# Two expert stages: all experts for all tokens, against 46 tiles of tokens sorted by expert

## The chip, the cores and the metric

The kernel runs on one core of a Trainium2 chip. The metric is the device time of one execution in microseconds. A core has five engines that each work through their own instruction stream: TensorE (PE, with its weight loads shown apart as PEld), VectorE (DVE), ScalarE (ACT), GpSimd (POOL) and SyncE (SP, which here only issues DMAs). They are ordered against each other by semaphores alone.

## The reference

The reference is a network of eight stages on a residual of 4 batches of 1024 tokens of 128 features: attention, experts, a Mamba block, experts again, a sparse attention, a feed-forward stage, a delta-rule attention and a feed-forward stage. The change concerns the second and the fourth, which use the same weights:

```
logits = einsum('bsh,eh->bse', x, router_w)              # E = 8 experts, H = 128
probs = softmax(logits)
weights, indices = top_k(probs, 2)                       # K = 2 of 8
weights = weights / (weights.sum(-1) + 1e-06)
h13 = einsum('bsh,ehi->bsei', x, w13)                    # w13: 8 x 128 x 512
gate, up = split(h13, 2)                                 # 256 each
h = silu(gate) * up
y = einsum('bsei,eih->bseh', h, w2)                      # w2: 8 x 256 x 128
out = (take(y, indices) * weights).sum(over the 2)
```

Here x is the layer-normed residual, and the result is added to the residual. The reference computes all eight experts and uses two.

## The kernel before

The residual lies in SBUF as 32 tiles of 128 tokens (tokens on partitions). Each stage is a function that opens a block with one program for each engine; a stage ends when all engines have reached the end of its block. Operands of large products are split into two fp16 halves, high and low, and a product is three matmuls (`product_of_halves`, L246): high by high, high by low, low by high.

In `moe_stage` the work unit is a chunk of 512 tokens and one expert: 8 chunks x 8 experts = 64 units. `schedule()` yields one list of named pieces, and every engine walks through that same list and does the pieces that it knows; so the order on each engine is written out by hand, and the waits inside the pieces only delay. A unit j has these pieces. `up` (twice, for the two blocks of 128 hidden features): TensorE writes the gate and the value (6 matmuls of 512 columns each time), ScalarE takes Silu of the gate (L1226), VectorE multiplies it with the value into `exact` (L1313). `keep`: ScalarE rounds `exact` to the high half (L1234), GpSimd subtracts for the low half (L1250). `down`, two units later: TensorE makes 24 matmuls of 128 columns with token rows as output, and VectorE adds each tile of 128 tokens, scaled by the token's weight for this expert (zero for six of eight), to the residual (L1324). Between the units of a chunk, `ahead` places the preparation of the next batch: moments, root, norm (`apply`, L327), transposes (`turn`, L431, L416, L1214, L1261), router logits (L1158, L1277, L1278) and the choice of two experts (`choose`, L1281 to L1305), and for the first experts the split of their weights (L1201, L1267). Three buffers hold `exact`, gate and hidden halves.

At the start of the kernel, SP loads the first batch, the constants and the attention weights and then, in `load_rest`, the rest of the input, `expert_rank` and `router` (L84 to L86). The transfers that build attention's stacks follow it on the same queue: psi (L654), phi (L661, L669), the halves of q and k (L676), and the stacks (L691). GpSimd issues indirect DMAs in one place, the sparse stage (L2424), each with one row index for each of 128 partitions.

## Time and profile before

| | us |
|---|---|
| median of 3 runs | 3946.96 (3943.35 to 3953.65) |
| profiled execution, span from first to last instruction | 3942.5 |
| mean granted clock of TensorE in it | 0.872 |
| PE busy | 3249.7 (82%) |
| DVE busy | 2818.9 (72%) |
| ACT busy | 2313.5 (59%) |
| POOL busy | 1237.5 (31%) |

The page gives no time for the profiled execution other than its span; the median of the runs is 4.5 us above it. The page also cuts the span into 40 slices; the expert stages are the two stretches in which TensorE's digit is 9 and its granted clock 9 (slices 9 to 11, and 18 to 20). A busy share is the time an engine's instructions take; a granted clock of 1.00 is TensorE at 2.4 GHz, of 0.50 at 1.2 GHz, and values between are a mean of the two levels over the stretch.

### The profile page before, as it was taken

What the parts mean: (1) busy time and instruction counts of PE and PEld (TensorE: products, weight loads), DVE (VectorE), ACT (ScalarE), POOL (GpSimd) and SP (SyncE); (2) the same over time, 40 slices, a digit from 0 to 9 for tenths busy, and PEclk for the clock granted to TensorE, in tenths of its full rate; (3) what the DMA queues carried; (4) which work ended last, traced back from release to release, by engine and by line L of the source; (5) the groups of instructions that cost most, each with busy time, mean ns of one, the idle gap of its engine ahead of it and who ended that gap; (6) DMA issues with size and microseconds to landing.
All of it is one profiled execution on the core that took longest, in us unless ns stands there. A gap on an engine that the chain in (4) does not pass through costs nothing. (4 is left out here: it accounts for less than half of the span.)

```text
span 3942.5 us, 87849 instructions
## 1 busy us (share of the span) xinstructions
PE 3249.7 (82%) x36196; PEld 1488.6 (38%) x36256; DVE 2818.9 (72%) x4293; ACT 2313.5 (59%) x3870; POOL 1237.5 (31%) x1018
## 2 busy tenths in 40 slices
PE   6999999899867677689988888887995676776799
PEld 1222222266411122156533333333453555554445
DVE  8898899587679998887746767655445667656643
ACT  3888888766444555266542566665655564543565
POOL 1100100055436776645533000001004565452100
PEclk7999999999967778799999999998997676656799
...
DMA packets 136019, 84.34 MB, mean 21 GB/s; under 512 B 92386, under 2 KB 107539, under 8 KB 135491
## 3 DMA queue, kind: packets, MB, share of 16 engines
...
q10 hardware_dynamic: 64, 0.07, 0.0%
...
## 5 line engine op out<-in xcount | busy, mean ns | idle before, releaser
L989 DVE TENSOR_REDUCE attn_peak_halves<-attn_ps 128x2 f32<-128x1024 f32 x512 | 601.5, 1218 | 58.5 <-PE attn_ps L820 50.7
L942 ACT ACTIVATE attn_weights<-attn_ps 128x512 f32<-128x512 f32 x1024 | 531.0, 601 | 101.4 <-PE attn_ps L848 101.3
L2974 DVE TENSOR_REDUCE sparse_peak<-sparse_ps 128x4 f32<-128x1024 f32 x256 | 309.6, 1223 | 136.3 <-PE sparse_ps L2600 134.5
L1250 POOL TENSOR_TENSOR moe_hidden<-moe_exact,moe_hidden 128x512 f16<-128x512 f32 x256 | 296.7, 1162 | 330.7 <-ACT moe_hidden L1234 322.0
L3672 POOL TENSOR_TENSOR delta_q<-delta_q,delta_weighted 128x512 f32<-128x512 f32 x240 | 324.1, 1377 | 235.4 <-ACT delta_weighted L4066 235.3
L2827 ACT ACTIVATE sparse_weights<-sparse_ps 128x512 f32<-128x512 f32 (+1 forms) x512 | 272.0, 585 | 173.8 <-PE sparse_ps L2667 87.9
L246 PE MATMUL moe_ps<-moe_xT_halves,moe_w_halves 128*128 128x512 f16 x1536 | 363.8, 384 | 9.4 <-DVE moe_w_halves L1267 5.9
L1772 POOL TENSOR_TENSOR mamba_out_c<-mamba_states,mamba_c_rep 128x1024 f32<-128x1024 f32 x128 | 301.4, 2367 | 176.8 <-DVE mamba_states L1839 138.5
L848 PE MATMUL attn_ps<-attn_q_stack,attn_k_stack 50*128 50x512 f16 x1024 | 321.9, 386 | 29.9 <-ACT attn_weights L942 7.1
L246 PE MATMUL ffn_ps<-ffn_layers,ffn_h_halves 128*128 128x512 f16 x1536 | 334.5, 379 | 3.6 <-ACT ffn_gate L3219 3.6
L1558 PE MATMUL mamba_ps<-mamba_stack,mamba_spread 96*128 96x512 bf16 x512 | 196.2, 493 | 157.3 <-ACT mamba_decays L1726 85.7
L1839 DVE TENSOR_TENSOR_SCAN mamba_states<-mamba_decays,mamba_ps 128x1024 f32<-128x1024 f32 x128 | 292.7, 2287 | 26.3 <-ACT mamba_decays L1726 10.1
L820 PE MATMUL attn_ps<-attn_k_stack,attn_q_stack 48*128 48x512 f16 x1024 | 271.2, 396 | 13.9 <-DVE attn_peak_halves L989 12.6
L3291 DVE TENSOR_TENSOR ffn_layers<-ffn_exact,ffn_layers 128x512 f16<-128x512 f32 x192 | 132.5, 692 | 204.8 <-ACT ffn_layers L3208 204.3
L860 PE MATMUL attn_ps<-attn_weights,attn_values 128*9 128x512 f32 x2048 | 270.3, 600 | 0.0
L1726 ACT ACTIVATE mamba_decays<-mamba_ps,mamba_rates 128x1024 f32<-128x1024 f32 x128 | 141.9, 1113 | 179.4 <-PE mamba_ps L1558 177.4
L1226 ACT ACTIVATE moe_gate<-moe_ps 128x512 f32<-128x512 f32 x256 | 152.0, 594 | 138.4 <-PE moe_ps L246 134.4
L1313 DVE SCALAR_TENSOR_TENSOR moe_exact<-moe_ps,moe_gate 128x512 f32<-128x512 f32 x256 | 174.5, 684 | 78.4 <-ACT moe_gate L1226 72.4
L848 PEld LDWEIGHTS attn_ps<-attn_q_stack,attn_k_stack 50*128 50x128 f16 x1024 | 80.6, 94 | 375.1 <-ACT attn_weights L942 284.4
L246 PEld LDWEIGHTS ffn_ps<-ffn_layers,ffn_h_halves 128*128 128x128 f16 x1536 | 149.9, 98 | 184.4 <-issue 4.5
L246 PE MATMUL moe_ps<-moe_w_halves,moe_hidden 128*128 128x128 f16 x3072 | 193.7, 220 | 18.2 <-POOL moe_hidden L1250 13.6
L246 PEld LDWEIGHTS moe_ps<-moe_xT_halves,moe_w_halves 128*128 128x128 f16 x1536 | 145.0, 99 | 164.5 <-DVE moe_w_halves L1267 8.0
...
## 6 DMA issues: line engine op xcount, KB each, us to landing
mamba_stack<-mamba_parts SPq DMA_DIRECT2D x96, 128.0 KB, 2.4
...
attn_q_stack<-attn_peak_rows SPq DMA_DIRECT2D x128, 2.0 KB
```

The lines of the kernel that those rows point to most:

```text
L246: made = pe.matmul(out, a, b, start=first and i == 0, stop=last and i == 2)
L820: made = pe.matmul(use.slot[:, p, :], q_stack[rows, slot, couple, t * P:(t + 1) * P], k_stack[rows, slot, couple, half_of(keys)], start=Tr ...
L848: pe.matmul(use.slot, k_stack[rows, slot, couple, k * P:(k + 1) * P], q_stack[rows, slot, couple, half_of(half)], start=True, stop=True).t ...
L860: made = pe.matmul(out_acc[32 * h:32 * h + HD + 1, :], values[:, b % 2, k, first + h, :], weights[:, step_no(g, half, k) % 2, h, :], start ...
L942: act.activation(weights[:, at % 2, h, :], use.slot, ACT.Exp).then_inc(*key_act.one())
L989: dve.tensor_reduce(peak_halves[:, turn % PEAKS, keys, at:at + 2], use.slot, AX_X, ALU.max).then_inc(*score_dve.one())
L1250: pool.tensor_tensor(low, exact_sb[:, i % 3, :], hidden[:, i // EB % 3, i % EB, 0, :], ALU.subtract).then_inc(*hidden_low.one())
L1772: pool.tensor_tensor(out_c[:, n % PRODUCTS, :], states[:, n % HELD, :], c_rep[:, b % 2, :], ALU.mult).then_inc(*product_made.one())
L1839: dve.tensor_tensor_scan(states[:, n % HELD, :], decays[:, n % DECAYS, :], mine, 0.0, ALU.mult, ALU.add).then_inc(*scanned.one())
L2827: act.activation(weights[:, at % 2, h, begin:], use.slot[:, begin:], ACT.Exp).then_inc(*key_act.one())
L2974: dve.tensor_reduce(peak[:, at % PEAKS, unit // 2, 4 * r:4 * r + 4], use.slot.rearrange("p h (a k) -> p (h a) k", a=2), AX_X, ALU.max).the ...
L3672: pool.tensor_tensor(so_far, so_far, weighted[:, half, :], ALU.add).then_inc(*long_added.one())
```

## The change

The two expert stages compute each token only for its two experts. In each stage:

- All four batches are prepared before the first product (`prepare`): norm, transposes, logits and choice as before, and `halve` makes a row of 256 fp16 values (high and low half) for each token. Batches 0 and 1 form lot 0, batches 2 and 3 lot 1 (`LOTS`).
- `rank` counts, by matmuls of the membership matrix with a triangular and a full matrix of ones, how many tokens of each expert stand before each token of the lot. `place_lot` turns this into a slot number for each token's first and second choice, where each expert's list begins at a multiple of 256, and into a table of which expert each tile of 256 slots belongs to. A lot has 2 x 2048 / 256 + 7 = 23 tiles, whatever the counts, so 46 in all.
- GpSimd writes the rows to `sorted_x` in HBM, by one indirect DMA for each 128 tokens and choice (32 for each lot, 64 in all).
- A tile j: SP loads its 256 rows (6 buffers), TensorE turns them with an fp16 identity (4 matmuls of 128 columns), ScalarE copies them, TensorE reads the expert's address from the table into a register (`value_load`) and makes 12 matmuls of 256 columns and, two steps later, 12 of 128 columns, all with the weights `parts` addressed by that register. ScalarE does Silu, the high half and the copy of the result; VectorE the product and the low half (which was GpSimd's); SP stores 256 result rows of fp32 to `sorted_y`.
- When all tiles of a lot are stored, GpSimd gathers each token's two result rows (again 64 indirect DMAs in all), and VectorE adds them, scaled, to the residual (`combine`).
- `load_rest` zeroes both lists `sorted_x` once, at the start of the kernel. Two constants are loaded at the start of each expert stage. The semaphores `zeroed`, `scattered` and `gathered` are the kernel's own for its whole length.

```diff
         sp.dma_start(self.router[:], self.dram["router"]).then_inc(*self.rest_in.dma())
+        for lot in self.sorted_x:
+            n = lot.shape[0] // SLOTS_E
+            sp.dma_start(lot.rearrange("(n p s) d -> p n (s d)", p=P, s=SB), self.dram["e_zeros"].unsqueeze(1).broadcast_to(
+                [P, n, SB * 2 * P])).then_inc(*self.zeroed.dma())
...
+SB = SLOTS_E // P
+LOTS = ((0, 2), (2, 4))
+PER_EXPERT = 2 * HIDDEN_E * 2 + EB * P * 2
+LOW13, HIGH2, LOW2 = 2 * HIDDEN_E, 4 * HIDDEN_E, 4 * HIDDEN_E + EB * P
+LIMITS = 16
+lot_tiles = lambda g: (LOTS[g][1] - LOTS[g][0]) * T * 2 // SLOTS_E + EXPERTS - 1
+LOT_STARTS = [sum(lot_tiles(n) for n in range(g)) for g in range(len(LOTS) + 1)]
+MOE_TILES = LOT_STARTS[-1]
...
+        def prepare(b):
+
+            yield "apply", b, 0
+            yield "turn", b, 0
+            yield "apply", b, 1
+            yield "turn", b, 1
+            yield "halve", b
+            yield "logits", b
+            yield "raise", b
+            yield "choose", b, 0
+            yield "choose", b, 1
+            if b + 1 == LOTS[lot_of(b)][1]:
+                yield "rank", lot_of(b)
+                yield "place", lot_of(b)
+            yield "weigh", b
...
+            early = [b for b in range(B) if lot_of(b) < 2]
+            for n, b in enumerate(early):
+                yield from prepare(b)
+                if n == 0:
+                    for other in range(1, B):
+                        yield "moments", other, 0
+                        yield "moments", other, 1
+                        yield "root", other
+                for e_ in range(n * EXPERTS // len(early), (n + 1) * EXPERTS // len(early)):
+                    yield "split", e_
+            late = [piece for b in range(B) if lot_of(b) >= 2 for piece in prepare(b)]
+            yield "gather_tile", 0
+            total_steps = MOE_TILES + 4
+            for j in range(total_steps):
+                if 1 <= j <= MOE_TILES:
+                    yield "high", j - 1
+                if 3 <= j < MOE_TILES + 3:
+                    yield "keep", j - 3
+                if j + 1 < MOE_TILES:
+                    yield "gather_tile", j + 1
+                if 1 <= j <= MOE_TILES:
+                    yield "low", j - 1
+                if j < MOE_TILES:
+                    yield "up", j
+                if 2 <= j < MOE_TILES + 2:
+                    yield "down", j - 2
+                if late and j >= 1:
+                    yield late.pop(0)
+                if j == LOT_STARTS[2] + 2:
+                    for c in range(HALVES * LOTS[0][0], HALVES * LOTS[0][1]):
+                        yield "combine", c
+            for c in range(HALVES * LOTS[0][1], CHUNKS):
+                yield "combine", c
+                if c == HALVES * TAKEN - 1:
                     yield ("next_root",)
                     yield ("next_inverse",)
...
+                def load(j):
+                    g = lot_of_tile(j)
+                    at = (j - LOT_STARTS[g]) * SLOTS_E
+                    if j == LOT_STARTS[g]:
+                        sp.wait_ge(*scattered[g].at(16 * 2 * span(g)))
+                    if j >= LOADED:
+                        sp.wait_ge(*turned_tile.at(j - LOADED + 1))
+                    sp.dma_start(sorted_in[:, j % LOADED], net.sorted_x[g][at:at + SLOTS_E].rearrange(
+                        "(p s) d -> p s d", s=SB)).then_inc(*loaded[j % LOADED].dma())
+
+                def store(j):
+                    g = lot_of_tile(j)
+                    at = (j - LOT_STARTS[g]) * SLOTS_E
+                    sp.wait_ge(*y_taken.at(j + 1))
+                    sp.dma_start(net.sorted_y[g][at:at + SLOTS_E].rearrange("(p s) d -> p s d", s=SB),
+                                 y_sb[:, j % STORED]).then_inc(*stored[j % STORED].dma())
+
+                for j in range(MOE_TILES + LOADED):
+                    if j < MOE_TILES:
+                        load(j)
+                    if j >= LOADED:
+                        store(j - LOADED)
+                for n in range(STORED):
...
+                def gather_tile(j):
+                    if j == 0:
+                        pe.wait_ge(*prepared.at(1))
+                    pe.wait_ge(*loaded[j % LOADED].at(16 * (j // LOADED + 1)))
+                    if j:
+                        pe.wait_ge(*taken.at(j))
+                    for half in range(2):
+                        for s in range(SB):
+                            at = half * SLOTS_E + s * P
+                            made = pe.matmul(ps[:, 0, at:at + P], sorted_in[:, j % LOADED, s, half * P:(half + 1) * P],
+                                             ident_half[:], start=True, stop=True)
+                    made.then_inc(*turned_tile.one())
...
+                def up(j):
+                    g = lot_of_tile(j)
+                    if j == 0:
+                        pe.wait_ge(*weights_low.at(2 * EXPERTS))
+                    if j == LOT_STARTS[g]:
+                        pe.wait_ge(*tabled.at(g + 1))
+                    value[j] = pe.value_load(expert_at[0:1, j:j + 1], min_val=0, max_val=(EXPERTS - 1) * PER_EXPERT)
+                    pe.wait_ge(*taken.at(j + 1))
+                    source = sorted_T[:, j % 2, 0, :], sorted_T[:, j % 2, 1, :]
+                    for which, (bank, empty, full) in enumerate(((gate_bank(j), gated, gate_full),
+                                                                 (value_bank(j), exact_made, value_full))):
+                        if j >= 2:
+                            pe.wait_ge(*empty.at(j - 1))
+                        for k in range(EB):
+                            at = which * HIDDEN_E + k * P
+                            made = product_of_halves(pe, bank[:, k * SLOTS_E:(k + 1) * SLOTS_E],
+                                                     (parts[:, bass.ds(value[j] + at, P)],
+                                                      parts[:, bass.ds(value[j] + (LOW13 + at), P)]), source)
+                        made.then_inc(*full.one())
...
+                def gather_tile(j):
+                    act.wait_ge(*turned_tile.at(j + 1))
+                    if j >= 2:
+                        act.wait_ge(*value_full.at(j - 1))
+                    act.copy(sorted_T[:, j % 2].rearrange("p h n -> p (h n)"), ps[:, 0, :]).then_inc(*taken.one())
+
+                def up(j):
+                    if j >= 2:
+                        act.wait_ge(*exact_made.at(j - 1))
+                    act.wait_ge(*gate_full.at(j + 1))
+                    act.activation(gate_sb[:, j % 2, :], gate_bank(j), ACT.Silu, scale=1.0 / W_SCALE).then_inc(*gated.one())
+
+                def high(j):
+                    if j >= KEPT:
+                        act.wait_ge(*out_full.at(j - KEPT + 1))
+                    act.wait_ge(*exact_made.at(j + 1))
+                    act.copy(hidden[:, j % KEPT, 0].rearrange("p k n -> p (k n)"),
+                             exact_sb[:, j % 2, :]).then_inc(*hidden_high.one())
+
+                def keep(j):
+                    act.wait_ge(*out_full.at(j + 1))
+                    if j >= STORED:
+                        act.wait_ge(*stored[j % STORED].at(16 * (j // STORED)))
+                    act.copy(y_sb[:, j % STORED].rearrange("p s d -> p (s d)"), out_bank).then_inc(*y_taken.one())
+
+                pieces = {"root": lambda b: norm.root(act, b), "prepare_consts": prepare_consts, "split": split, "turn": turn,
+                          "halve": halve, "raise": raise_, "gather_tile": gather_tile, "up": up, "high": high, "keep": keep,
+                          "next_root": lambda: norm.root_next(act)}
                 for piece, *at in schedule():
                     if piece in pieces:
                         pieces[piece](*at)
 
...
             def _(pool):
-                for i in range(EB * units):
-                    pool.wait_ge(*hidden_high.at(i + 1))
-                    low = hidden[:, i // EB % 3, i % EB, 1, :]
-                    if i // EB >= 3:
-                        pool.wait_ge(*out_full.at(i // EB - 2))
-                    pool.tensor_tensor(low, exact_sb[:, i % 3, :], hidden[:, i // EB % 3, i % EB, 0, :],
-                                       ALU.subtract).then_inc(*hidden_low.one())
+                def scatter(b):
+                    g = lot_of(b)
+                    pool.wait_ge(*tokens_low.at(b + 1))
+                    pool.wait_ge(*placed.at(g + 1))
+                    for t in range(b * TPB, (b + 1) * TPB):
+                        for k in range(2):
+                            pool.indirect_dma_start(net.sorted_x[g], bass.IndirectOffsetOnAxis(slot_at[:, k, t:t + 1], 0),
+                                                    rows[:, t].rearrange("p h d -> p (h d)"),
+                                                    None).then_inc(*scattered[g].dma())
+
+                def gather(c):
+                    g = lot_of(c // HALVES)
+                    if c == HALVES * LOTS[g][0]:
+                        for n in range(STORED):
+                            pool.wait_ge(*stored[n].at(16 * len(range(n, LOT_STARTS[g + 1], STORED))))
+                    for t in range(c * TPC, (c + 1) * TPC):
+                        for k in range(2):
+                            pool.indirect_dma_start(found[:, t, k, :], None, net.sorted_y[g], bass.IndirectOffsetOnAxis(
+                                slot_at[:, k, t:t + 1], 0)).then_inc(*gathered[c].dma())
+
+                pool.wait_ge(*net.zeroed.at(16 * len(LOTS)))
+                for b in range(B):
+                    scatter(b)
+                for c in range(CHUNKS):
...
+                def place_lot(g):
+                    n, tiles = span(g), slice(LOTS[g][0] * TPB, LOTS[g][1] * TPB)
+                    limits = steps_in[:, 0:LIMITS].unsqueeze(1).broadcast_to([P, EXPERTS, LIMITS])
+                    counts = rank_bank(g)[:, n * EXPERTS:]
+                    before = rank_bank(g)[:, 0:n * EXPERTS].rearrange("p (t e) -> p t e", e=EXPERTS)
+                    dve.wait_ge(*ranked.at(g + 1))
+                    if g == 0:
+                        dve.wait_ge(*consts_in.at(32))
+                    settle(dve.tensor_tensor(over[:], counts.unsqueeze(2).broadcast_to([P, EXPERTS, LIMITS]), limits, ALU.is_gt))
+                    settle(dve.tensor_reduce(ends[:, 0, :], over[:], AX_X, ALU.add))
+                    settle(dve.tensor_tensor_scan(ends[:, 1, :], ones[:], ends[:, 0, :], 0.0, ALU.mult, ALU.add))
+                    settle(dve.tensor_tensor(ends[:, 2, :], ends[:, 1, :], ends[:, 0, :], ALU.subtract))
+                    made = dve.scalar_tensor_tensor(place[:, tiles], ends[:, 2, :].unsqueeze(1).broadcast_to([P, n, EXPERTS]),
+                                                    float(SLOTS_E), before, ALU.mult, ALU.add)
+                    made.then_inc(*based.one())
+                    dve.wait_ge(*based.at(g + 1))
+                    for k, picks in enumerate((chosen, runner)):
+                        settle(dve.tensor_tensor(key[:, tiles], picks[:, tiles], place[:, tiles], ALU.mult))
+                        settle(dve.tensor_reduce(slot[:, k, tiles], key[:, tiles], AX_X, ALU.add))
+                    dve.tensor_copy(slot_at[:, :, tiles], slot[:, :, tiles]).then_inc(*placed.one())
+                    lot, m = slice(LOT_STARTS[g], LOT_STARTS[g + 1]), lot_tiles(g)
+                    settle(dve.tensor_tensor(passed[:, lot], ends[0:1, 1, :].unsqueeze(1).broadcast_to([1, m, EXPERTS]),
...
+                def low(j):
+                    dve.wait_ge(*hidden_high.at(j + 1))
+                    dve.tensor_tensor(hidden[:, j % KEPT, 1].rearrange("p k n -> p (k n)"), exact_sb[:, j % 2, :],
+                                      hidden[:, j % KEPT, 0].rearrange("p k n -> p (k n)"),
+                                      ALU.subtract).then_inc(*hidden_low.one())
+
+                def combine(c):
+                    dve.wait_ge(*gathered[c].at(16 * 2 * TPC))
+                    for k in range(2):
+                        for t in range(c * TPC, (c + 1) * TPC):
+                            x = net.residual[:, t, :]
+                            made = dve.scalar_tensor_tensor(x, found[:, t, k, :], share[:, k, t:t + 1], x, ALU.mult, ALU.add)
+                        made.then_inc(*added.one())
+                        dve.wait_ge(*added.now())
+                    if c < HALVES * TAKEN:
+                        norm.take_next_moments(dve, c)
```

## Rows read from the trace of the kernel before

**Rows 1.** The page, busy us (share of the span) and instructions of each engine.
```profile
PE 3249.7 (82%) x36196; PEld 1488.6 (38%) x36256; DVE 2818.9 (72%) x4293; ACT 2313.5 (59%) x3870; POOL 1237.5 (31%) x1018
```

**Rows 2.** Timeline, first expert stage's edges: start, duration, instruction, idle before it.
```profile
765.61 0.35 SPq L1140 DMA_DIRECT2D moe_w<-in_w  x1
...
768.77 2.14 DVE L327 TENSOR_SCALAR moe_xn<-residual,w_ln_moments,w_ln_inv 128x128 f32<-128x128 f32 x8
...
772.39 0.57 ACT L416 COPY moe_xT<-moe_ps 128x512 f32<-128x512 f32 x1
...
773.26 4.58 PE L246 MATMUL moe_ps<-moe_xT_halves,moe_w_halves 128*128 128x512 f16 x12 [1.19 <-DVE moe_xT_halves L1261]
...
1054.32 0.34 SPq L1536 DMA_DIRECT2D mamba_w_in<-in_m_w_in  x1
```

**Rows 3.** Busy us of each engine in a stretch, clock, DMA share, GB/s.
```profile
855.00:955.00 100.00, 95.71 (x865) 61.26 (x864) 78.78 (x221) 65.83 (x112) 55.97 (x49) 1.00 0.01 1
```

**Rows 4.** Timeline of one unit in the steady state.
```profile
1041.60 1.50 PE L246 MATMUL moe_ps<-moe_w_halves,moe_hidden 128*128 128x128 f16 x24
1042.94 2.75 PE L246 MATMUL moe_ps<-moe_xT_halves,moe_w_halves 128*128 128x512 f16 x12
1045.53 1.50 PE L246 MATMUL moe_ps<-moe_w_halves,moe_hidden 128*128 128x128 f16 x24
...
1043.14 1.13 DVE L1324 SCALAR_TENSOR_TENSOR residual<-moe_ps,moe_weights,residual 128x128 f32<-128x128 f32 x4 [0.54 <-PE moe_ps L246]
1043.85 0.60 ACT L1226 ACTIVATE moe_gate<-moe_ps 128x512 f32<-128x512 f32 x1 [1.52 <-PE moe_ps L246]
1044.55 0.69 DVE L1313 SCALAR_TENSOR_TENSOR moe_exact<-moe_ps,moe_gate 128x512 f32<-128x512 f32 x1 [0.27 <-ACT moe_gate L1226]
```

**Rows 5.** Instructions by line (ns min/median/max, first and last start), and one of the timeline.
```profile
L1214 ACT ACTIVATE moe_xT_halves<-moe_xT x16: 629/630/631, 771.9 to 1865.8; 128x512 f16<-128x512 f32 x16
...
L980 DVE TENSOR_TENSOR attn_phi_parts<-attn_sums,attn_phi_parts x1: 1226/1226/1226, 14.6 to 14.6; 128x1024 f16<-128x1024 f32 x1
...
770.83 1.02 DVE L1267 SCALAR_TENSOR_TENSOR moe_w_halves<-moe_w,moe_w_halves 128x512 f16<-128x512 f32 x2
```

**Rows 6.** Small VectorE operations of the choice by line; norms, grouped (busy us, mean ns).
```profile
L1282 DVE TENSOR_TENSOR moe_key<-moe_probs,moe_total x8: 828/1056/1066, 785.2 to 1876.9; 128x64 f32<-128x64 f32 x8
L1282 DVE TENSOR_TENSOR moe_key<-moe_left,moe_second x8: 224/225/226, 787.9 to 1881.8; 128x64 f32<-128x64 f32 x8
...
L327 DVE TENSOR_SCALAR moe_xn<-residual,w_ln_moments,w_ln_inv 128x128 f32<-128x128 f32 x32 | 14.5, 514 | 0.1
```

**Rows 7.** GpSimd's indirect DMAs in the sparse stage; their landing; a 128 KB DMA.
```profile
2083.20 1.12 POOL L2424 DMA_INDIRECT sparse_gathered_k<-sp_table_k,sparse_row_at  x1 [15.09 <-DVE sparse_row_at L2966]
2084.62 0.99 POOL L2424 DMA_INDIRECT sparse_gathered_v<-sp_table_v,sparse_row_at  x1 [0.30 <-issue]
2085.59 6.58 POOL L2415 DMA_DIRECT2D sparse_k_stack<-sp_halves  x12
...
DMA to landing us min/median/max: 2.7/2.8/3.8
...
mamba_stack<-mamba_parts SPq DMA_DIRECT2D x96, 128.0 KB, 2.4
```

**Rows 8.** A ScalarE copy of 128 columns out of PSUM.
```profile
L927 ACT COPY attn_bias_row<-attn_ps x1: 278/278/278, 25.8 to 25.8; 128x128 f32<-128x128 f32 x1
```

**Rows 9.** Busy us by stretch as in rows 3: Mamba stage, sparse stage.
```profile
1200.00:1300.00 100.00, 71.97 (x228) 16.13 (x228) 91.20 (x57) 55.26 (x53) 75.77 (x34) 0.74 0.07 16
...
2200.00:2300.00 100.00, 87.18 (x1072) 34.15 (x1085) 66.97 (x56) 68.13 (x134) 7.72 (x23) 0.98 0.04 11
```

**Rows 10.** Start of the kernel: router load, first attention scores, busiest DMA stretch.
```profile
12.94 0.43 SPq L86 DMA_DIRECT2D w_router<-in_router  x1
...
38.70 0.61 PE L820 MATMUL attn_ps<-attn_k_stack,attn_q_stack 48*128 48x512 f16 x2
...
6.00:17.00 11.00, 5.32 (x12) 2.94 (x13) 7.95 (x27) 3.92 (x6) 0.38 (x1) 1.00 0.91 267
```

318 lines of the change are left out of this document (151 added, 167 removed).

## The prediction

> **What bounds the kernel now.** I read the page first: TensorE is busy 82% of a 3942.5 us span and no other engine comes near it over the whole [rows 1]. A whole-kernel share says nothing about two stages out of eight, so next comes the timeline at their edges. The first expert stage runs from 765.61 to the first DMA of the stage after it at 1054.32, 288.7 us [rows 2]; the second repeats the pattern from 1675.67 to 1964.92, 289.3 us. The first product of an expert begins at 773.26, so only 7.65 us are preparation. The busy times of the stretch 855 to 955 show the steady state: TensorE 95.7 of 100 us at a granted clock of 1.00, VectorE 79, ScalarE 66, GpSimd 56 [rows 3]. The timeline of a unit (one chunk of 512 tokens, one expert) repeats every 1045.53 - 1041.60 = 3.93 us, with 24 products of 128 columns in 1.50 us and 12 of 512 in 2.75 us, back to back [rows 4]. 64 units of 3.93 are 251 us. TensorE alone bounds these stages; the other engines fit inside its time.
>
> **What the change removes.** All 8 experts are computed for all 4096 tokens now, and two are used. Afterwards 46 tiles of 256 tokens are computed. Per tile there are 12 products of 256 columns, 12 of 128 and 4 of 128 (turning the loaded rows). A product of 512 columns takes 2.75/12 = 0.229 us and one of 128 takes 1.50/24 = 0.0625 [rows 4]; halfway by columns, 256 costs 0.118. The tile is 12 x 0.118 + 16 x 0.0625 = 2.41 us, and 46 tiles are 111 us of TensorE in place of 251. The 140 us saved are the whole gain. The rest of this part is what is paid for them, in the order of the stage.
>
> **Preparation, now in front of everything.** Lot 0 needs batches 0 and 1 normed, routed and ranked before a single token can be placed, where the kernel before prepares batches 1 to 3 beside the products. Up to the first applied norm it is as now, 3.16 us (765.61 to 768.77) [rows 2]. A batch then runs serially: 8 norms 2.14 us; from their end to the copy of the turned half 2.05 us (770.91 to 772.96) [rows 2, 5]; the high half of 1024 columns on ScalarE, twice the 0.63 of 512, 1.26; the low half on VectorE 1.23; two operations on logits 0.5, Exp with its hop 0.35, and 15 small operations of the choice at 0.225 plus about 0.04 between them, 3.9 [rows 5, 6]. That is 11.5. To it come the weighing of batch 0 (4 small operations, 1.0), the moments of three batches (2.4 each, which is 3.16 less 0.7 for root and reciprocal, 7.2), two experts' weights split (1.02 each on VectorE, 2.0) [rows 5], batch 1 (11.5), the ranking by 17 small products (1.5), and place_lot up to its slots, 10 settled operations of 64 to 128 elements at about 0.3 (3.0). Sum 3.2 + 11.5 + 1.0 + 7.2 + 2.0 + 11.5 + 1.5 + 3.0 = 40.9 us. The logits' products on TensorE lie beside the halving. The 1.5 and the 3.0 are estimates from those small operations, good to a microsecond.
>
> **Scatter.** 32 indirect DMAs of GpSimd place lot 0. The trace has eight, in four pairs: from start to start 1.42 us in two of them, 1.32 in the others, of which 0.99 to 1.12 is the instruction and 0.30 lies between the two; they land after 2.8 [rows 7]. The rows moved there are twice as long, the count of 128 rows is the same. I take 1.37: 32 x 1.37 = 43.8 us. Bounds: 0.97, the time from the second of a pair to the plain DMA behind it, and 2.2, which is 1.37 with the 0.83 us added that a small VectorE operation took more beside GpSimd (1056 ns against 225) [rows 6]. At 0.97 the stage gains 26 us on this forecast, if nothing else holds it, and at 2.2 it loses 27. All of it is on the path, since the first tile waits for the whole lot's semaphore. Then 2.8 to land, 0.35 to issue the load and 2.4 for 128 KB [rows 2, 7], 1.0 for turning and copying: 40.9 + 43.8 + 6.6 = 91.3 us. Nothing of the tiles can start earlier. What VectorE does meanwhile (batches 2 and 3, the other six experts, about 39 us) ends near 80 us and is hidden, and would come out only if the scatter took less than about 33 us. Lot 1's 32 scatters (to about 129 us) and lot 0's 32 gathers lie beside tiles and cost nothing, unless GpSimd is late by over 40 us.
>
> **Pace of a tile.** TensorE could do 2.41 us. ScalarE now has four operations: 0.60 for Silu, 0.63 for the high half, 0.57 for the copy of the turned rows, about 0.38 for the result's 256 columns (between 0.28 for 128 and 0.57 for 512) [rows 2, 4, 5, 8]. But in its order `high` of tile j-1 comes first in step j, and it waits for VectorE's product, which waits for the Silu that ScalarE did last. The cycle is Silu 0.60, hop 0.10 (1044.45 to 1044.55), product 0.69, hop 0.10, high 0.63, result copy 0.38, turned copy 0.57, and 0.03 between each of four: 3.2 us. The rings of three to six buffers don't break it, since it is an order on one engine. Below it lies 2.41. Above it lies TensorE at its lower clock: 5120 columns at 1.2 GHz are 4.27 us, 4.5 with the issue. The granted clock was 0.74 where TensorE was busy 72% and 0.98 at 87% [rows 9]; at 2.41 of 3.2, 75%, the new stage lies between these. Each tile also loads a register from SBUF on TensorE's queue and addresses 24 operands by it, which no row of this trace prices; by the nearest bounds it costs nothing while TensorE's 0.8 us of slack hide it, and the pace is 4.5 when they don't. I take 3.5, a tenth over the cycle and nearest to it. 46 tiles and three steps of drain: 49 x 3.5 = 171.5 us, to 262.8.
>
> **After the last tile.** Its store takes 2.8 (issue and 128 KB), then lot 1's 32 gathers 43.8, all exposed because the first waits for every store of the lot; 2.8 to land and 8 combining operations 2.3, from four in 1.13 [rows 4]. 262.8 + 51.7 = 314.5 us, against 288.7 and 289.3: slower by 25.5 a stage, 51 for both. Residual additions of the kernel before (256 operations of 0.34 per stage) become 64, and GpSimd's 128 subtractions go to VectorE; neither bounded and neither will.
>
> **The zeroed lists.** 46 tiles x 256 rows x 512 B = 6.03 MB are written at the start on SP's queue, behind the router's load (its DMA is issued at 12.94 us) and ahead of psi, phi and the stacks that the first scores need (38.70) [rows 10]. The busiest stretch moved 267 GB/s at 0.91 of the queues, so it takes 23 us. The DMAs behind it were issued from 13.4 to 30.1 with waits in between; redone behind a queue that is free at 36, the stacks land near 47 to 52, 8 to 14 us after 38.70. Bounds: 0, if the small transfers find a way around, and 26, if HBM to HBM runs at half the rate. I take 14. The second stage pays nothing here.
>
> **Sum.** 51 + 14 = 65 us. The profiled execution has a span of 3942.5; the page gives no time around it, and the median of the three timed runs is 3947.0, 4.5 above. On the span the sum is 4008, as a time 4012 us.
>
> One rule of the Trainium skill speaks against this change. Rows first: a small VectorE operation on 64 columns took 1056 ns where its twin took 225, and the norms of 128 columns took 514 ns in the mean in a stage where GpSimd is busy half the time, against 0.27 a piece in the first eight, before GpSimd begins [rows 2, 6]. SBUF — State Buffer, "Who interferes with whom", says that VectorE in its two-port modes (copy, cast, tensor_scalar) takes the port pair it shares with GpSimd for the whole instruction, and that a DMA of GpSimd is then starved of descriptor time. The norms of batches 2 and 3 are tensor_scalar, and run beside lot 0's scatter. The trace agrees as far as it shows the two engines holding each other up; it has no indirect DMA beside a norm. By that rule the scatter would go as in the last rival below; without it, 1.37 stands.
>
> **The rivals.**
> - Tile pace set by TensorE's queue (register loads, register addresses, the lower clock): 4.5 us a tile. For it: the clock of 0.74 at 72% busy, and the serial waits of the queue. Against: 0.98 at 87% [rows 9]. 49 x 1.0 more per stage, 98 for both: 4110 us.
> - The other side: TensorE keeps the pace, 2.41 us, as it does now at clock 1.00. For it: GpSimd and VectorE are light in the tiles, and TensorE has been the one bound of the stage [rows 3]. Against: the ScalarE cycle, written out above, which needs ScalarE to do two tiles at once. 49 x 1.09 less, 107 for both: 3905 us. Faster begins at a pace of 3.5 - 65/98 = 2.84 us.
> - Indirect DMAs of 2.2 us in the first scatter, where VectorE prepares beside it: 32 x 0.83 = 27 a stage, 53 for both: 4065 us. For it: [rows 6]. Against: the low count of two-port operations, 16 norms and a few copies in those 44 us.
>
> **How the numbers follow.** The forecast gets 0.45, with a range of its own of 3970 to 4060 (pace 3.18 to 3.9, zeros 0 to 26); TensorE's queue 0.18; the other side 0.24; slow scatters 0.10; 0.03 lies within 0.3%, about what a measurement of this kernel can tell from no change. Range 3900 to 4115: down to the fast case, up to the slow one, which leaves out the combinations of several costs and any bigger gain. Faster 0.25, same 0.03, slower 0.72.
>
> **What would show it.** In the changed profile: first product of an expert about 91 us after the stage's first DMA (right if 80 to 100); DMA_INDIRECT 128 times a stage with 1.3 to 1.4 between starts and 32 of them after the last store; Silu to Silu 3.2 to 3.9 us with ScalarE's `high` waiting for VectorE; granted clock of the tiles between 0.6 and 1; first scores at 47 to 53 us. The prediction is wrong if Silu to Silu is under 2.84, if a gather or scatter costs well under 1 us, or if the loads of registers show as TensorE waiting a microsecond or more in each tile.

## The result, and the profile of the changed kernel

| | time (us) | ratio to before, 95% interval |
|---|---|---|
| before | 3947.57 (3943.35 to 3953.65) | |
| changed | 4087.11 (4079.35 to 4094.62) | 1.0355 [1.0334, 1.0376] |

Forecast was 4012, so the sign was right, and the forecast cost, 65 us, was under half of the 139.5 measured. The page of the changed kernel, beside [rows 1]: TensorE has shed 245 us of work and the span is 135 us longer.

```profile
span 4077.5 us, 84371 instructions
...
PE 3005.2 (74%) x34232; PEld 1387.9 (34%) x34292; DVE 2653.2 (65%) x3877; ACT 2174.6 (53%) x3696; POOL 1190.8 (29%) x1018
```

The first expert stage now runs from SP's first DMA at 774.53 to that of the Mamba stage at 1126.34, 351.8 us against 288.7 [rows 2]; the second from 1750.02 to 2104.70, 354.7 against 289.3. GpSimd's timeline gives the edges of its four bursts of 32 indirect DMAs (only the first of each burst is shown; within one, nearly all starts are 1.25 to 1.27 apart, a few up to 1.76, and the last ones start at 858.99, 909.57, 1020.08 and 1117.25):

```profile
818.46 1.21 POOL L1370 DMA_INDIRECT sorted_x<-moe_rows,moe_slot_at  x1 [87.31 <-DVE moe_slot_at L1472]
...
870.30 0.96 POOL L1370 DMA_INDIRECT sorted_x<-moe_rows,moe_slot_at  x1 [10.34 <-DVE moe_slot_at L1472]
...
980.50 1.42 POOL L1381 DMA_INDIRECT moe_found<-sorted_y,moe_slot_at  x1 [69.97 <-DMA sorted_y<-moe_y]
...
1078.21 0.95 POOL L1381 DMA_INDIRECT moe_found<-sorted_y,moe_slot_at  x1 [57.18 <-DMA sorted_y<-moe_y]
```

Busy times cut at these edges and at the tiles' own (columns as in [rows 3]: length, busy us of PE, PEld, DVE, ACT, POOL, granted clock, DMA share, GB/s):

```profile
774.50:818.50 44.00, 12.49 (x65) 10.98 (x65) 30.08 (x145) 14.57 (x25) 0.04 (x1) 0.50 0.24 74
818.50:861.00 42.50, 11.40 (x48) 9.84 (x48) 15.98 (x53) 6.14 (x11) 32.01 (x32) 0.50 0.16 50
861.00:881.50 20.50, 9.42 (x76) 7.37 (x77) 10.77 (x39) 6.06 (x11) 8.70 (x9) 0.57 0.24 72
881.50:915.50 34.00, 4.76 (x22) 1.76 (x19) 1.40 (x2) 1.81 (x4) 22.09 (x23) 0.56 0.15 46
915.50:986.00 70.50, 62.58 (x699) 52.78 (x700) 35.54 (x52) 48.24 (x102) 4.40 (x4) 0.95 0.32 98
986.00:1025.00 39.00, 4.47 (x34) 2.37 (x31) 1.83 (x3) 2.27 (x5) 26.67 (x28) 0.61 0.20 56
1025.00:1078.00 53.00, 43.70 (x480) 36.83 (x480) 28.29 (x56) 33.97 (x71) 0.00 (x0) 0.92 0.27 84
1078.00:1122.50 44.50, 0.00 (x0) 0.00 (x0) 20.96 (x93) 0.31 (x1) 30.53 (x32) 0.50 0.18 47
```

The fourth and sixth lines are the finding. Lot 1's scatters lie in 881.5 to 915.5 and lot 0's gathers in 986 to 1025, and there hardly any engine but GpSimd works: TensorE 4.8 of 34 us and 4.5 of 39. Between them TensorE is busy 62.6 of 70.5. TensorE's timeline of the first band shows how it goes on, for long nothing and then one product at a time, waiting for nothing that the profile shows ("issue"):

```profile
881.06 0.84 PE L251 MATMUL moe_ps<-moe_parts,moe_hidden 128*128 x8
883.08 0.22 PE L251 MATMUL moe_ps<-moe_parts,moe_hidden 128*128 x1 [1.18 <-issue]
883.81 0.22 PE L251 MATMUL moe_ps<-moe_parts,moe_hidden 128*128 x1 [0.51 <-issue]
885.22 0.22 PE L251 MATMUL moe_ps<-moe_parts,moe_hidden 128*128 x1 [1.19 <-issue]
887.34 0.26 PE L251 MATMUL moe_ps<-moe_parts,moe_hidden 128*128 x1 [1.91 <-issue]
901.44 0.59 PE L1261 MATMUL moe_ps<-moe_ident_half,moe_sorted_in 128*128 128x128 f16 x4 [13.84 <-issue]
...
907.73 0.37 PE L251 MATMUL moe_ps<-moe_sorted_T,moe_parts 128*128 128x256 f16 x1 [2.44 <-issue]
910.52 0.37 PE L251 MATMUL moe_ps<-moe_sorted_T,moe_parts 128*128 128x256 f16 x1 [2.42 <-issue]
```

The single products start about 0.70 us or a multiple of it apart (0.73, 1.41, 2.12 and 2.79 in these lines), where those of 256 columns are 0.11 apart in the steady tiles. But a large part of each band is one standstill: 13.84 us here, and 28.26 in front of the product at 1025.31 in the second. The others wait for TensorE. The same thing stands in the first burst, with no tile, no register and no load of SP's near it. TensorE's products for batch 3's logits start between 840.48 and 843.67 and their signal (a semaphore event of the trace) comes at 860.74, 0.8 us after the burst's last DMA; VectorE, which waits for it, stands 18.23 us (the releaser printed had long been done):

```profile
841.31 1.23 DVE L1409 TENSOR_TENSOR moe_rows<-moe_xn,moe_rows 128x1024 f16<-128x1024 f32 x1 [2.83 <-ACT moe_rows L1324]
860.76 0.23 DVE L1419 TENSOR_REDUCE moe_best<-moe_ps 128x8 f32<-128x64 f32 x1 [18.23 <-DMA attn_sums<-in_tables]
```

So these products had started by the trace, and what is missing is their end. The band has it too. The four products that turn tile 3 start at 879.04; their signal stands in the trace at 900.68, 21.3 us after the recorded end of the last of them, where it comes 0.01 after it in the steady tiles, and ScalarE's copy, which waits for it, starts at once:

```profile
879.04 0.39 PE L1261 MATMUL moe_ps<-moe_ident_half,moe_sorted_in 128*128 128x128 f16 x4
900.71 0.59 ACT L1334 CAST moe_sorted_T<-moe_ps 128x512 f16<-128x512 f32 x1 [6.34 <-remote]
```

Away from bursts a tile repeats every 929.88 - 927.19 = 2.69 us. ScalarE's timeline shows the cycle of the prediction, with `high` waiting 0.81 for VectorE's product:

```profile
927.19 0.61 ACT L1340 ACTIVATE moe_gate<-moe_ps 128x512 f32<-128x512 f32 x1
928.61 0.62 ACT L1346 CAST moe_hidden<-moe_exact 128x512 f16<-128x512 f32 x1 [0.81 <-DVE moe_exact L1486]
929.14 0.37 ACT L1353 COPY moe_y<-moe_ps 128x256 f32<-128x256 f32 x1
929.40 0.59 ACT L1334 CAST moe_sorted_T<-moe_ps 128x512 f16<-128x512 f32 x1
929.88 0.61 ACT L1340 ACTIVATE moe_gate<-moe_ps 128x512 f32<-128x512 f32 x1
```

And the zeroed lists move the first scores from 38.70 [rows 10] to:

```profile
45.31 1.03 PE L825 MATMUL attn_ps<-attn_k_stack,attn_q_stack 48*128 48x512 f16 x4 [6.62 <-DMA attn_k_stack<-attn_halves]
```

That is not their whole cost. The expert stage behind attention starts 8.9 us later than before (774.53 against 765.61). In the other runs that zero at the start it is 5.9 to 19.0 us (771.51 to 784.65), and none in those that don't, or that do it later (763.70 to 765.38).

### The profile page after: what moved, and what is told of

Its sections match the earlier page's. It is cut to its first block and busy times, and to the rows that moved or that the text cites. A ratio compares the mean times of both kernels' runs of the same rounds, so it can differ in the third digit from the quotient of the medians.

```text
span 4077.5 us, 84371 instructions
## 1 busy us (share of the span) xinstructions
PE 3005.2 (74%) x34232; PEld 1387.9 (34%) x34292; DVE 2653.2 (65%) x3877; ACT 2174.6 (53%) x3696; POOL 1190.8 (29%) x1018
## 5 line engine op out<-in xcount | busy, mean ns | idle before, releaser
L3465 DVE TENSOR_TENSOR ffn_layers<-ffn_exact,ffn_layers 128x512 f16<-128x512 f32 x192 | 132.7, 692 | 204.7 <-ACT ffn_layers L3382 204.2
L1381 POOL DMA_INDIRECT moe_found<-sorted_y,moe_slot_at x128 | 123.5, 965 | 291.9 <-DMA sorted_y<-moe_y 254.1
L4240 ACT ACTIVATE delta_weighted<-delta_v,delta_fir_w 128x512 f32<-128x512 f32 x240 | 168.7, 721 | 61.9 <-POOL delta_q L3846 61.0
L251 PE MATMUL moe_ps<-moe_sorted_T,moe_parts 128*128 128x256 f16 x1104 | 153.0, 289 | 59.5 <-issue 48.3
L1486 DVE SCALAR_TENSOR_TENSOR moe_exact<-moe_ps,moe_gate 128x512 f32<-128x512 f32 x92 | 63.6, 692 | 204.3 <-ACT moe_gate L1340 139.7
L1370 POOL DMA_INDIRECT sorted_x<-moe_rows,moe_slot_at x128 | 125.0, 976 | 203.9 <-DVE moe_slot_at L1472 166.1
L771 POOL TENSOR_SCALAR attn_peak_parts<-attn_peak 128x16 f16<-128x16 f32 x32 | 8.3, 261 | 550.5 <-DVE attn_peak L1000 550.5
```

The source lines that it names most:

```text
L251: made = pe.matmul(out, a, b, start=first and i == 0, stop=last and i == 2)
```

## The experiments

Every run edits the changed kernel or repeats a kernel unchanged, but for bursts_row and bursts_plain, which edit the kernel before. The theory: a burst of back-to-back indirect DMAs of GpSimd holds the other engines up. Rivals: the register-addressed weights, the traffic, the tiles' own order. Each run names the chip that it ran on, which came to matter. The kernel before took a median between 3944.6 and 3949.2 us on all six chips, so it doesn't tell them apart. The chip of the first measurement above isn't recorded; it shows the bands.

### Chip 1: take the overlap away, or the register

**serial** keeps everything of GpSimd's away from tiles.

```
-  if j == LOT_STARTS[g]:
-      sp.wait_ge(*scattered[g].at(16 * 2 * span(g)))
+  if j == 0:
+      for lot in range(len(LOTS)):
+          sp.wait_ge(*scattered[lot].at(16 * 2 * span(lot)))
...
-  if c == HALVES * LOTS[g][0]: ...  # lot g stored
+  if c == 0: ...                    # all tiles stored
```

> Nothing of GpSimd's lies beside tiles any more: tile 0's load waits for both lots' 64 scatters, and all 64 gathers wait for the last store. Theory (a burst of back-to-back indirect DMAs holds the other engines up, so that what lies beside it gains nothing): both bands of about 36 us without tiles go, two bands of 40.5 us of exposed scatters and 40 us of exposed gathers come; a stage is 96 + 40.5 + 5.5 + 49 x 2.69 + 3 + 80 + 5 = 362 us against 348, so about 4115 us. Rival (the bands come from the tiles' own order, from the change of lots or from the buffers): they stay and the exposed DMAs are added, 4240 us or more. By the prediction's own belief (bursts beside tiles cost nothing) it would be 4087 + 2 x 80 = 4247 us.

4115.79 us, ratio 1.0432 [1.0401, 1.0464], as the theory had it (4115). All 46 tiles run in one stretch, TensorE busy 114 of 138 us, and none of it is lost:

```profile
860.00:917.00 57.00, 1.22 (x17) 1.14 (x17) 9.64 (x38) 1.91 (x5) 37.65 (x40) 0.50 0.14 45
917.00:1055.00 138.00, 114.06 (x1288) 95.89 (x1288) 63.66 (x92) 89.52 (x186) 1.24 (x3) 0.95 0.29 90
1055.00:1140.00 85.00, 0.00 (x0) 0.00 (x0) 19.97 (x88) 0.00 (x0) 59.80 (x63) 0.50 0.19 49
```

Putting 64 DMAs per stage (81 us) beside tiles had gained 29 us for two stages, not 160. The tiles' order and buffers are cleared.

**static** makes the weight addresses constants.

```
-  value[j] = pe.value_load(expert_at[0:1, j:j + 1], ...)
+  value[j] = (j % EXPERTS) * PER_EXPERT
```

> TensorE's weight addresses are constants (expert j mod 8 for tile j): it loads no register, and the tiles do not use the weights of their tokens' expert. Rival (register loads and addressed operands are what is slow beside the bursts): the bands without tiles go, about 3940 us, tiles keep their 2.7 us pace beside the bursts. Theory (the bursts hold up whatever the engines run): the bands stay as long as they were, 36 us each, and the time is 4087 within 10 us, because the register instructions were hidden in the steady pace.

4068.97 us, 1.0314 [1.0285, 1.0342], 18 less than the changed kernel, where I had allowed 10. The bands stay. The windows below are those of the changed kernel, and this stage starts 7.1 us later, so they catch some of the running tiles. Fairer is what the starts of Silu are apart beyond 2.69 us, summed over a stage: 68 us here, 74 in the changed kernel. Registers account for at most the 18 us gained, 9 a stage, about 6 of them in the bands.

```profile
881.50:915.50 34.00, 8.12 (x63) 5.20 (x60) 3.46 (x5) 4.02 (x8) 25.93 (x27) 0.59 0.19 59
986.00:1025.00 39.00, 8.92 (x65) 5.54 (x63) 3.71 (x6) 4.76 (x9) 27.55 (x29) 0.60 0.25 68
```

### Chip 1: pace the bursts

**paced2** and **paced6of8** make each pair wait for the Silu of one more tile; **passed_waits** adds a wait that is always met; **spaced4** puts a memset of 0.95 us behind every fourth DMA.

```
   for t in ...:
+      pool.wait_ge(*gated.at(t - 15))                    # paced2, lot 1's scatters
+      pool.wait_ge(*gated.at(t - 15 + (t - 16) // 3))    # paced6of8
+      pool.wait_ge(*placed.at(1))                        # passed_waits
       for k in range(2):
           pool.indirect_dma_start(...)
+      if t % 2: settle(pool.memset(idle[:], 0.0))        # spaced4
```

> GpSimd waits for ScalarE's silu of one more tile ahead of every two indirect DMAs of lot 1's scatters and of lot 0's gathers: 2.5 us of DMA in each 2.69 us tile, so a gap of 0.2 us only. Theory: the engines are held up only while GpSimd issues without a pause, and a wait that follows their progress cannot run them dry for 30 us; if a gap of 0.2 us is enough, the two bands of about 36 us go and the time is about 3940 us; if a gap must be longer, tiles and DMAs take turns, and it is between 3990 and 4087 us. Rival (the DMAs' traffic makes the tiles' loads late): the rate of the traffic is nearly the same, so the time stays within 20 us of 4087.

> As the one before with every fourth tile left free: six DMAs and then a pause of about 3 us, 32 DMAs over 21 tiles. Theory (a pause lets the others catch up): no band without tiles, a stage of 348 - 75 = 273 us, 3937 us in all, less than before the change (3947). If six DMAs in a row are already too many: some us lost in each run of six, 3960 to 4040 us. Rival (traffic): three quarters of the rate, still some 60 us lost of 150, about 4030 us.

> The changed kernel with a semaphore wait of GpSimd ahead of each pair of indirect DMAs that is always met already: the bursts stay as dense, only their instruction stream is broken by a wait every 2.5 us. If the paced kernels were cured by the break in the stream (an instruction between the DMAs at which GpSimd lets others go), the bands without tiles vanish here too: about 3945 us. If they were cured by the pauses or by GpSimd following the tiles, the time stays at 4087 within 15 us.

> The changed kernel with a GpSimd memset of 0.95 us (own tile) after every four indirect DMAs, in all bursts: pauses that follow nobody's progress. A burst of 32 takes 32 x 1.26 + 8 x 1.2 = 50 us instead of 40. If a pause of about 1 us every 5 us is what the others need, the two bands of 36 us per stage go (-150 us) and the exposed bursts grow (first scatters and last gathers 10 us each, twice: +40 us): about 3975 us. If the feedback from the tiles is needed (GpSimd waiting when they fall behind), the bands stay and grow with the burst: about 4087 + 40 + 20 = 4150 us.

paced2 3988.90 (1.0111 [1.0078, 1.0143]), paced6of8 3991.52 (1.0111 [1.0089, 1.0134]): 98 and 96 us gained. passed_waits 4086.25 (1.0350 [1.0303, 1.0396]): nothing. spaced4 4026.12 (1.0197 [1.0148, 1.0247]): 61 gained, between the 3975 and the 4150 that I expected, though the pauses lengthen the four exposed bursts by 28 (46 to 47 us in place of 39 to 41). So the break must be a pause, not an instruction. That one which follows the tiles does better isn't shown: the paced bursts also paused more (32 DMAs in 57.4 and 52.2 us in paced2, 47 in spaced4, 39 to 40 unbroken).

The rival of traffic predicted 4087 within 20 for paced2 on the ground of an equal rate. The rate came out a quarter to a third lower, so this run alone doesn't rule it out. A loss in proportion to the rate would be some 110 of the 147 us of the bands, though, and 50 are left; and chip 5 below carries the same rows at full rate without loss. Both paced kernels missed the 3940 of the theory. In paced2 every second or third tile beside the pairs loses mostly 1.4 to 2.4 us (Silu 905.18 to 910.16 against 2.69), 24 and 26 us a stage:

```profile
902.50 0.61 ACT L1340 ACTIVATE moe_gate<-moe_ps 128x512 f32<-128x512 f32 x1
905.18 0.61 ACT L1340 ACTIVATE moe_gate<-moe_ps 128x512 f32<-128x512 f32 x1
910.16 0.62 ACT L1340 ACTIVATE moe_gate<-moe_ps 128x512 f32<-128x512 f32 x1
```

### The same bursts beside the dense stages

GpSimd issues 64 row DMAs beside the tiles of each dense stage (static addresses, no loads). bursts_row: rows of the input, index 0 everywhere, in the second dense stage with an operation of GpSimd after every four; bursts_plain: not indirect, in the second dense stage issued by SyncE. Both edit the kernel before. real_rows edits the changed kernel: the expert stage's slots, gathers from the result lists in the first dense stage and scatters in the second.

```
+  for n in range(64):
+      pool.indirect_dma_start(fetched[:, n, :], None, table, IndirectOffsetOnAxis(row_at[:, 0:1], 0))    # bursts_row
+      pool.dma_start(fetched[:, n, :], table[n * 16:n * 16 + P])                                        # bursts_plain
+      pool.indirect_dma_start(fetched[:, n, :], None, net.sorted_y[g], ...net.slot_at[:, k, t:t + 1])    # real_rows
```

> The kernel before, with 64 indirect row gathers of 128 rows of 512 B on the otherwise idle GpSimd beside the tiles of each dense stage (static weight addresses, no loads of the tiles' own; the fetched rows are not used): in the first dense stage back to back, in the second with one GpSimd elementwise operation of about 1.3 us after every four. Theory (back-to-back indirect DMAs starve TensorE of instructions, which come in blocks of 16 KB; a dense stage uses up some 12 TensorE instructions per us): TensorE runs on for 20 to 40 us and then all but stops until the burst of 80 us ends: 40 to 60 us lost in the first dense stage, under 10 us in the second: about 3997 us. Rival (only tiles with register-addressed weights, or tiles that load from DRAM, suffer): nothing lost in either, 3947 within 10 us. Rival (the traffic of the row DMAs is what disturbs): both stages lose, the second at four fifths of the rate nearly as much as the first.

> As the one before, other DMAs of the same bytes (128 rows of 512 B each, 64 of them back to back, consecutive rows, not used): in the first dense stage plain transfers issued by GpSimd, in the second the same transfers issued by SyncE on its own queue. If GpSimd's making of descriptors is the cause, the first dense stage loses as with indirect DMAs when they follow each other as closely (40 to 60 us), and the second nothing, about 3997 us; if it is the indirect form alone, neither loses, 3947 within 10 us; if it is the traffic of 64 KB every 1.3 us, the second stage loses as well, or more, since SyncE issues one every 0.4 us: over 3980 us.

> The changed kernel with bursts of 64 indirect DMAs beside the tiles of both dense stages, this time with the real slots of the second expert stage as rows: gathers of 512 B rows in the first dense stage, scatters of 512 B rows in the second (results unused). In the run before, with every index 0, TensorE kept its full pace beside such a burst for 80 us. If what holds TensorE up in the expert stages is the kind of rows (distinct rows spread over DRAM, packets that land within 3 us), the dense stages now lose 30 to 60 us each: 4087 + 60 to 120 = about 4170 us. If it is something of the expert stages' own code (instruction rate, its many waits), the dense stages lose under 10 us: about 4095 us.

bursts_row (chip 9) 3956.24, 1.0015 [0.9996, 1.0033]; bursts_plain (chip 9) 3947.16, 0.9994 [0.9978, 1.0011]; real_rows (chip 1) 4240.12, one run, 153 us over the changed kernel. Its first dense stage, from the burst's start at 2902.73 to its end at 2983:

```profile
2903.00:2923.00 20.00, 18.51 (x84) 7.96 (x83) 6.33 (x22) 7.06 (x11) 15.43 (x16) 1.00 0.20 50
2923.00:2983.00 60.00, 11.64 (x27) 2.52 (x25) 3.68 (x18) 6.49 (x9) 45.37 (x49) 0.54 0.19 52
2983.00:2988.00 5.00, 1.16 (x3) 0.23 (x3) 0.75 (x1) 0.00 (x0) 0.42 (x1) 0.56 0.07 21
2988.00:3020.00 32.00, 28.85 (x159) 14.11 (x159) 15.76 (x30) 20.17 (x31) 0.00 (x0) 0.86 0.00 1
```

The bands are no property of the expert stages: 20 us into a burst nearly everything stops here too. The DMA engines are 0.19 busy meanwhile, so it is no lack of bandwidth. In bursts_row they were 0.90 busy (128 reads of one row land after 15.9 us) and TensorE worked through:

```profile
2750.00:2785.00 35.00, 33.23 (x155) 14.87 (x153) 19.34 (x60) 23.43 (x35) 26.77 (x28) 1.00 0.86 41
2785.00:2830.00 45.00, 45.00 (x289) 24.32 (x288) 22.71 (x40) 28.90 (x44) 34.09 (x36) 1.00 0.90 40
```

I took this for proof that distinct rows decide. It was not: between the two runs the rows, the table, the kernel around them and the chip had changed.

### Which chip

**zero_rows** and **real_gaps** were to separate row, table, form and gap. Both are the changed kernel with other bursts in the dense stages (index 0 of the result lists, then plain transfers; the real slots with a short GpSimd operation after every second, then after every eighth gather), and their expert stages are unchanged, with unbroken bursts of 32.

> The changed kernel with 64 row DMAs beside the tiles of each dense stage again. First dense stage: indirect gathers from the same result lists as in the run that stopped everything, but with index 0 in all rows. Second: plain transfers issued by GpSimd that read 128 distinct rows, 16 KB apart, from these lists. If distinct rows matter only with the indirect form, neither stage loses, 4087 within 15 us. If distinct, scattered rows through GpSimd's queue are enough in any form, the second loses 20 to 60 us. If it was the table (lists in DRAM that the kernel itself owns, not an input) and not the index, the first loses about 75 us.

> The changed kernel with 64 indirect gathers by the real slots beside the tiles of each dense stage, and a small GpSimd operation with its semaphore (a gap of some 0.7 us) after every second gather in the first dense stage, after every eighth in the second. Unbroken, such bursts cost the two dense stages 153 us in all. If a gap of 0.7 us lets the engines through, whoever's progress it follows, a gap every 2.5 us cures the first (loss under 10 us) and one every 10 us leaves part of the loss in the second (10 to 60 us): 4110 to 4150 us. If only waiting for the tiles cures, both lose 70 us or more: 4230 us or more.

Chip 5: zero_rows 3928.00, real_gaps 3932.26 (one run each; before 3944.58 there). Both are below the kernel before, with 128 extra DMAs, which no row of the expectations allowed. Their expert stages have no bands. In zero_rows the first burst starts at 828.26, the first tile's Silu at 877.06, the last burst at 1005.72, and the stage lasts 269.3 us (784.34 to 1053.67), 19.4 less than before:

```profile
828.00:869.00 41.00, 12.61 (x65) 10.97 (x65) 25.59 (x92) 8.04 (x16) 31.29 (x32) 0.50 0.16 49
869.00:875.00 6.00, 1.13 (x8) 0.70 (x8) 0.00 (x0) 0.59 (x1) 4.57 (x5) 0.50 0.53 163
875.00:1005.50 130.50, 112.96 (x1281) 95.31 (x1280) 68.62 (x114) 88.81 (x185) 61.62 (x60) 0.97 0.40 120
1005.50:1053.50 48.00, 0.00 (x0) 0.00 (x0) 20.72 (x92) 0.31 (x1) 30.36 (x32) 0.50 0.17 44
```

In the third line 60 indirect DMAs lie beside tiles and the pace is 2.69 throughout. real_gaps loses nothing in its dense stages either. Here are 70 us of the second, inside the burst with the real slots, where eight gathers at a time follow each other unbroken:

```profile
3736.00:3806.00 70.00, 68.23 (x397) 34.67 (x394) 35.96 (x77) 46.36 (x69) 53.77 (x62) 1.00 0.22 59
```

The queues of 883 to 915, first the changed kernel, then zero_rows: the same 736 packets of GpSimd's DMAs, and beside them nothing in the one; 3168 packets of loads and stores and four blocks of instructions in the other.

```profile
q0 software_dynamic: 736, 1.51, 15.1%
```

```profile
q1 hardware_dynamic: 3168, 2.88, 30.5%
q0 software_dynamic: 736, 1.51, 14.2%
q8 instruction: 4, 0.07, 1.1%
```

If the chip decides, the same kernel must differ from chip to chip. So unchanged kernels ran again:

> The changed kernel, unchanged, once more. All runs in which the engines stopped beside bursts of indirect DMAs were on one chip (serial, static, paced2, paced6of8, real_rows, passed_waits, spaced4); none of those on two other chips showed a stop anywhere, not even beside 32 unbroken scatters in their expert stages (zero_rows, real_gaps). If the stop belongs to a chip and not to a kernel: on the first chip 4087 again within 15 us, on any other about 3928 us (what zero_rows took, whose 128 extra DMAs were hidden), so faster than before. If it belongs to the kernel's code or memory layout, 4087 on every chip.

> The changed kernel, unchanged, a third time, to meet a chip of the other kind: so far chips 1 and 7 stop beside bursts of row DMAs (4087, 4080 here; the kernel of four lots 3997 on chip 7), chips 5 and 9 do not (the kernel of four lots 3893 on both). On chip 5, 9 or another without stops about 3925 us, 0.5% less than before the change; on a chip with stops 4080 within 15 us.

> The changed kernel a fourth time, for a chip of the other kind (1, 7 and 14 stop beside bursts, 5 and 9 did not). On a chip without stops about 3925 us, on one with stops 4080 within 15 us.

> The kernel with 64 unbroken gathers and 64 unbroken scatters by real slots beside the dense stages' tiles, 4240 us on chip 1. On a chip without stops the bursts are hidden: about 3930 us. On one with stops 4240 within 20 us.

The changed kernel took 4080.27 on chip 7 (1.0339 [1.0310, 1.0368]), 4079.32 on chip 14 (1.0339 [1.0319, 1.0358]) and 4073.37 on chip 0 (1.0321 [1.0298, 1.0343]), with both bands each time; real_rows_again 4215.54 on chip 0. after_again had been expected at 3928 on any chip but chip 1, which chip 7 refutes. None of the three met a chip of the other kind. The evidence comes from the next kernel, which ran unchanged on one of each kind.

### Four lots

**four_lots** has one batch a lot, paces its pairs, and issues the zero fills in the middle of the attention stage; **four_unpaced** drops the pacing inside a batch; **four_again** is four_lots unchanged.

```
-LOTS = ((0, 2), (2, 4))
+LOTS = ((0, 1), (1, 2), (2, 3), (3, 4))
...
+  if piece == "spread" and at[0] < 2:
+      net.zero(sp, HALVES * at[0] + at[1])
...
+  scatter(0)
+  for what, b, first in ((scatter, 1, 1), (scatter, 2, 14), (gather, 0, 24), (scatter, 3, 33), (gather, 1, 43), (gather, 2, 52)):
+      beside = [first + t + t // 4 for t in range(TPB)]   # four_unpaced: [first] * TPB
```

> Built on the theory: one lot per batch (four lots, 60 tiles instead of 46), so that only 16 scatters stand ahead of the first tile and only 16 gathers behind the last; the other 96 indirect DMAs go in pairs, each pair waiting for the silu of a tile of its own (4 tiles of 5), and the four zero fills are issued in the middle of the attention stage instead of at its start. Theory: first product about 58 us after the stage's start, 60 tiles of 2.69 us and 15 to 25 us for TensorE's fetches that wait for a pause = 180 us, 3 + 20 + 5 us at the end: 266 us a stage against 288.7 before the change, and no 6.6 us at the start: about 3905 us, faster than before (3947). If the late batches' preparation and the pairs cost the tiles more than that (pace above 3.5 us), 3947 or more.

> The kernel with four lots, without pacing inside a batch: each of the six blocks of 16 indirect DMAs of a stage that lie beside tiles still starts at the same tile, but then runs without pause (20 us). Theory: the engines stop some 6 to 12 us into each block until it ends, 8 to 14 us and a refill of 3 us lost in each of 12 blocks: 3893 + 130 to 200 = about 4050 us. Rival (the gain of that kernel came from the lots alone, since they leave only 32 exposed DMAs): 3893 within 10 us.

> The kernel of four lots, paced, once more and on the same chip as the run beside it. On a chip without stops 3893 within 10 us. On the chip with stops its paced pairs lose some 1.4 us now and then, as in the paced kernels of two lots (15 to 25 us a stage), and its first 16 scatters delay little: 3930 to 3960 us.

four_lots on chip 9: 3893.19 (3891.69 to 3899.23), ratio 0.9859 [0.9835, 0.9882]. four_unpaced on chip 5: 3893.34, 0.9871 [0.9837, 0.9906]. four_again on chip 7: 3996.59 (3996.54, 3996.64), 1.0135 [1.0104, 1.0167], 37 above what I had expected of a chip with stops. One kernel, 103 us apart. The stretch 900 to 960 of its stage on chip 9, then on chip 7:

```profile
900.00:960.00 60.00, 53.00 (x619) 45.34 (x616) 30.75 (x45) 41.24 (x88) 38.82 (x37) 1.00 0.47 138
```

```profile
900.00:960.00 60.00, 45.68 (x479) 35.82 (x480) 29.11 (x64) 33.54 (x70) 29.97 (x29) 0.97 0.36 107
```

In this stretch the pace on chip 9 is 2.69, with GpSimd issuing two DMAs in four tiles of five; on chip 7 every second or third tile takes 4.2 to 5.4. The stage is 264.0 us (763.91 to 1027.95) on the one and 309.6 (765.19 to 1074.81) on the other. On a chip without stops pacing is worth nothing (four_unpaced), so my expectation of 4050 for it fell with the theory's "on every chip".

What stands: on four chips (1, 7, 14, 0) bursts of indirect DMAs stop TensorE, on two (9, 5) they don't. Chip 1 was met twice, half an hour apart, and stopped both times. Each of the others was met once, so that a property of the occasion (where memory was placed, what else ran) would look the same as one of the chip. On chip 9 no unbroken burst of real rows ran, only the paced pairs and index 0. Open: what differs; what holds TensorE (the missing instruction blocks can as well follow from its standing still, and the late signals of products that had started are not explained by a lack of instructions); whether the recording takes part, since every execution listed has a recorded span and clock; whether index 0 or a gap of 0.7 us would help on a chip with stops, since both ran only on chips without; and the changed kernel itself on a chip without stops. For that zero_rows is the nearest, its extra DMAs being hidden: about 3928, 0.4% under the kernel before.

## Why the prediction was wrong

**The step that failed** is "Lot 1's 32 scatters (to about 129 us) and lot 0's 32 gathers lie beside tiles and cost nothing". From the first product at 874.01 to the last lot's gathers at 1078.21 there are 204.2 us, where 49 steps of 2.69 and a store of 2.8 make 134.6: the two bands cost 69.6 a stage, 139 in all. I priced GpSimd's queue, and asked what waits for it, but not what it does to engines that wait for nothing from it. No row of before could show it: its eight indirect DMAs come in pairs, 2.4 us long [rows 7]. A bound from above was called for, the bursts' own 40 us each, and the range would have reached 4170. That 4087 lies inside the stated 3900 to 4115 is luck: the upper end stood for TensorE's queue at 4110, which cost nothing of the kind, and two errors of 79 and 139 us had opposite signs.

**The tile's pace** hid half of this. I took 3.5, and the cycle worked out to 3.2, because I added up ScalarE's durations and hops of 0.03. In the trace starts lie 0.53, 0.26 and 0.48 apart for operations of 0.62, 0.37 and 0.59: on one engine they overlap by about 0.1, and 1.42 + 0.53 + 0.26 + 0.48 = 2.69. The trace of before had it, a Silu of 0.60 us and the high half 0.49 after its start:

```profile
1035.99 0.60 ACT L1226 ACTIVATE moe_gate<-moe_ps 128x512 f32<-128x512 f32 x1 [1.52 <-PE moe_ps L246]
1036.48 0.62 ACT L1234 ACTIVATE moe_hidden<-moe_exact 128x512 f16<-128x512 f32 x1
```

The rest is the tenth that I laid on top. The pace is worth 49 x 0.81 = 39.7 a stage, 79 in all; at 2.69, below my break-even of 2.84, the kernel would have come out faster but for the bands, though not as the other side had it, by TensorE's 2.41. The mechanism was right: `high` waits for the product, TensorE isn't the bound.

**The other steps.** First product 99.5 us after the start against 91.3: preparation 43.9 against 40.9, and 16.7 us of standing in the first burst delay the split of the last experts, which I had ending at 80. In zero_rows, without that stop, the first product comes at 91.2 (875.57 after 784.34). Scatters 41.5 us plus landing against 43.8: mostly 1.265 a piece, not 1.37. The four DMAs issued during the 16 norms took 0.96 to 1.02 us (one that began ahead of them, beside the split of weights, 1.47) and the norms 2.14 and 2.31 for eight against 2.14 alone, so the rival of slow scatters fell. The Trainium skill's rule (SBUF — State Buffer, "Who interferes with whom") didn't show beside these norms. The 0.83 us of that rival were not the price of scatters: beside them the small operation that took 1056 ns in [rows 6] takes 0.22 (at 830.62). Gathers 40.0 against 43.8; from their end to the next stage 8.1 against 5.1, of which 4.1 is the change of stage that I had left out. Zeroed lists 8.9 at the end of attention (6.6 at the first scores) against 14. Register loads were hidden, and the rival of TensorE's queue (4.5 a tile) fell: static gains 9 a stage at the same steady pace.

**The sum by these**: stage one 314.5 + 8.2 + 29.9 - 3.8 + 3.0 = 351.8, stage two 354.7, so 77.5 over the forecast; zeros 5.1 under: 4012 + 77.5 - 5.1 = 4084, measured 4079 to 4095. On a chip without stops, zero_rows' stages of 269.3 and 269.1 are 90.6 under the forecast together, and its start is 18.7 late, 4.7 over: 4012 - 90.6 + 4.7 = 3926, and it took 3928. So without the stops the change gains some 12 to 17 us (3928 and 3932 against 3944.6, one execution each), and what was measured is mostly one kind of chip's answer to its bursts.
